# A mixture-of-experts stage behind a graph layer: its first norm moved ahead of the last edge sums, its first experts among the last dense pieces, and its later norms to the front of each VectorE step

## The reference

```python
edge_index = jnp.stack([src, dst])
xn = _layernorm(x, axis=-1)
x = x + gnn(xn, edge_index, edge_type, ...) + mix(xn[None], ...)[0]   # 2 graph layers; 4 transformer layers
x = x + ffn(_layernorm(x, axis=-1)[None], ...)[0]

def ffn(x, ...):                       # x: 3125 x 256
    all_out = experts(x)               # 4 experts: 256 -> 128 -> 64 -> 256, relu, biases eb1, eb2, eb3
    shared = shared_mlp(x)             # 256 -> 256 -> 128 -> 256, relu, biases sb1, sb2, sb3
    gates = softmax(x @ gW + gb)
    topv, topi = top_k(gates, 2)
    topw = softmax(topv)
    return shared + sum of the two chosen experts' outputs weighted by topw
```

## Time and profile before

| | before |
|---|---|
| median of 3 runs | 2031.78 us (2028.99 to 2034.85) |
| the profiled execution | 2034.2 us, span 2032.5 us |
| TensorE matmul busy | 1876.7 us (92%) |
| TensorE weight load busy | 1576.5 us (78%) |
| VectorE busy | 1260.0 us (62%) |
| ScalarE busy | 677.9 us (33%) |
| GpSimd busy | 1330.8 us (65%) |
| mean granted TensorE clock | 0.976 |

### The profile page before, as it was taken

One profiled execution on the slowest core, in us unless ns is written; L12 is line 12 of the kernel. 1 busy time (PEld: TensorE's weight loads), 2 busy tenths in 40 slices (PEclk: granted clock), 3 DMA queues, 4 the chain that ended last, 5 costly groups with the idle time before them and its releaser, 6 DMA issues.

```text
span 2032.5 us, 32105 instructions
## 1 busy us (share of the span) xinstructions
PE 1876.7 (92%) x10496; PEld 1576.5 (78%) x10496; DVE 1260.0 (62%) x3348; ACT 677.9 (33%) x1864; POOL 1330.8 (65%) x1324
## 2 busy tenths in 40 slices
PE   3989999998899999979999998798999999998878
PEld 2558888886788888759888787566888888888878
DVE  6775576566656556475567645487656566555666
ACT  5542343343234333333343333122222222223333
POOL 5777777777777777777777415776777777750000
PEclk9999999999999999999999989899999999998889
DMA  8677666667766666776666536667666666560000
GB/s 243 193 241 220 199 186 200 205 193 234 227 198 190 197 198 182 233 236 199 207 193 207 153 84 230 214 204 233 204 195 187 219 203 208 182 138 14 26 14 26
DMA packets 195288, 371.62 MB, mean 183 GB/s; under 512 B 37993, under 2 KB 126863, under 8 KB 195131
## 3 DMA queue, kind: packets, MB, share of 16 engines
q0 software_dynamic: 77376, 223.09, 38.7%
q1 hardware_dynamic: 93587, 127.50, 19.0%
q10 hardware_dynamic: 24168, 19.04, 3.2%
HBM read 305.39 MB, written 64.95 MB: 182 GB/s over the span
## 4 chain that ended last, share of the span: by engine, by line
PE 63%; POOL 13%; DVE 12%; issue 6%; DMA 3%; ACT 2%; DVEq 1%; SPq 0%; ACTq 0%
PE ps_seg L2469 12%; PE ps_down L2592 12%; PE ps_hid L2583 11%; POOL xg L906 9%; POOL rg L862 4%; PE ps_kv L2502 3%; PE ps_kv L2891 3%; PE ps_x L2547 3%; DMA xg<-h_rows,idx_tab 2%; PE ps_hid L3036 2%; PE ps_x L528 2%; DVE xg L1008 2%; PE ps_hid L2522 1%; PE ps_down L2620 1%; DVE xres L1948 1%
## 5 line engine op out<-in xcount | busy, mean ns | idle before, releaser
L906 POOL DMA_INDIRECT xg<-h_rows,idx_tab x416 | 430.9, 1036 | 140.3 <-issue 116.2
L906 POOL DMA_INDIRECT xg<-xn_rows,idx_tab x416 | 431.6, 1037 | 128.8 <-issue 122.5
L862 POOL DMA_INDIRECT rg<-relation_rows,idx_tab x416 | 430.6, 1035 | 129.4 <-issue 129.1
L2469 PE MATMUL ps_seg<-xg,hot 128*125 128x257 f32 x1664 | 428.5, 389 | 44.0 <-DVE xg L1008 43.6
L2583 PEld LDWEIGHTS ps_hid<-hT,wff 128*128 128x128 f32 x3200 | 385.1, 193 | 15.7 <-issue 7.1
L2583 PE MATMUL ps_hid<-hT,wff 128*128 128x125 f32 x3200 | 389.4, 276 | 1.6 <-ACT gT L2069 0.9
L2469 PEld LDWEIGHTS ps_seg<-xg,hot 128*125 128x125 f32 x1664 | 296.1, 190 | 102.4 <-DVE xg L1008 44.7
L2592 PE MATMUL ps_down<-wff,gT 128*125 128x256 f32 x1600 | 364.0, 381 | 0.0
L1008 DVE TENSOR_TENSOR xg<-xg,rg 128x512 f32<-128x512 f32 x416 | 285.8, 687 | 79.7 <-DMA xg<-h_rows,idx_tab 52.3
L2069 ACT ACTIVATE gT<-ps_hid,b1p 128x125 f32<-128x125 f32 x800 | 226.6, 367 | 319.9 <-PE ps_hid L2583 319.7
L2592 PEld LDWEIGHTS ps_down<-wff,gT 128*125 128x125 f32 x1600 | 295.4, 189 | 41.7
(11 more groups left out here) (367 smaller groups left out, 2424.2 us busy)
## 6 DMA issues: line engine op xcount, KB each, us to landing
second_relation_rows<-rg SPq DMA_DIRECT2D x104, 512.0 KB, 4.0
rg<-second_relation_rows SPq DMA_DIRECT2D x104, 512.0 KB, 4.2
wff<-L_mix_W ACTq DMA_DIRECT2D x8, 1024.0 KB, 7.9
rg<-relation_rows,idx_tab POOLq DMA_INDIRECT x416, 3.5
xg<-xn_rows,idx_tab POOLq DMA_INDIRECT x416, 3.2
xg<-h_rows,idx_tab POOLq DMA_INDIRECT x416, 3.7
h_rows<-rg SPq DMA_DIRECT2D x25, 112.0 KB
qrow<-h_rows ACTq DMA_DIRECT2D x25, 112.0 KB
```

The lines of the kernel that those rows point to most:

```text
L862: pool.indirect_dma_start(rg[:, k, :], None, rel_d, bass.IndirectOffsetOnAxis(ap=idx_tab[:, step, 1:2], axis=0))\
L906: pool.indirect_dma_start(xg[:, k, 0:D], None, rows, bass.IndirectOffsetOnAxis(ap=idx_tab[:, step, 0:1], axis=0))\
L2469: ins = pe.matmul(ps_seg[u // UW % 2][0:T, 0:AW], hot[:, s % HOTS, :], xg[:, s % RING, :], start=s % WIN == 0, stop=s % WIN == WIN - 1)
```

## The change

On VectorE, `last_norm(0)`, the norm of the first five tiles, is called before the flush of the last edge sums instead of behind `aside(8)`. After the loop of layers the order of what is left is `dense_beside(49)`, `(50)`, `logits(0)`, `shift_logits(0)`, `(51)`, `softmax(0)`, `(52)`, `top_two(0)`, `gates(0)`, `(54)`. The shared bias is added once to all four experts' biases (the two gate weights of a row sum to one), and `add_biases` loses its first addition; for that the expert biases are loaded to one contiguous place. In the step loop, `gates` (of the group whose tiles begin now), `last_stats`, `last_rows`, `logits` and `shift_logits` come before the step's gated rows; `gates` moves from j = 4 to the next j = 0, `logits` and `shift_logits` from j = 3 to j = 4; `softmax` and `top_two` stay at the end of j = 4.

On TensorE, `turn_last(0)` and `(1)` move before `aside(9)`; `turn_last(2)` to `(4)`, `shared_1(0)`, `experts_1(0)` and the first logits go between dense pieces 50 and 51, and pieces 52 to 54 into step s = 1. ScalarE follows the same order; it waits for the last weights before dense piece 50, and `exp_gates` stand before `columns_out` at j = 0 and before `hidden_2` at j = 4.

```diff
@@ load places
-        eb3_b = kx5p[0:T, 0:KC, 0:2 * D]
+        eb3_b = flat_k[0:T, 0:NX * D].rearrange("p (b n) -> p b n", b=KC)
+        eb3_all = flat_k[0:T, 0:NX * D].rearrange("p (e n) -> p e n", e=NX)
@@ VectorE, iteration
                 early()
                 aside(8)
-                if (lay, gi) == (L - 1, NG - 1):
-                    last_norm(0)
                 b.add_ffn(3)
@@ VectorE, early
                         if (lay, gi) == (L - 1, NG - 1):
+                            last_norm(0)
                             edges.flush()
@@ VectorE, behind the layers
             dense_beside(behind + 1)
+            softmax(0)
             dense_beside(behind + 2)
-            softmax(0)
             top_two(0)
+            gates(0)
             dense_beside(behind + 4)
-            gates(0)
@@ VectorE, step loop
-                last(dve.tensor_tensor(z, z, b2_b[:, :], ALU.add))
...
+            last(dve.tensor_tensor(eb3_all, eb3_all, b2_b[:, :].unsqueeze(1).broadcast_to([T, NX, D]), ALU.add))
             for s in range(1, NT + 2):
                 gi, j = last_part(s)
+                if j == 0 and 1 < gi <= NG:
+                    gates(gi - 1)
+                if gi < NG:
+                    if j == 0:
+                        last_stats(gi)
+                    if j == 1:
+                        last_rows(gi)
+                    if j == 4:
+                        logits(gi)
+                        shift_logits(gi)
                 if s <= NT:
                     gated_rows(s - 1)
                 if s > 1:
                     add_experts(s - 2)
                 if s <= NT:
                     add_biases(s - 1)
-                if gi < NG:
-                    if j == 0:
-                        last_stats(gi)
-                    if j == 1:
-                        last_rows(gi)
-                    if j == 3:
-                        logits(gi)
-                        shift_logits(gi)
-                    if j == 4:
-                        softmax(gi)
-                        top_two(gi)
-                        gates(gi)
+                if gi < NG and j == 4:
+                    softmax(gi)
+                    top_two(gi)
@@ ScalarE, iteration
                 aside(7)
+                if (lay, gi) == (L - 1, NG - 1):
+                    aside(8)
+                    last_turned(0)
+                    last_turned(1)
+                    aside(9)
+                    return
@@ ScalarE, behind the layers
-            last_turned(0)
-            last_turned(1)
+            last_turned(2)
+            last_turned(3)
+            act.wait_ge(s_ew, 16 * LAST_LOADS)
+            act.wait_ge(s_fo, L * NT + 1)
+            hidden_shared(0)
+            last_turned(4)
             dense_beside(behind)
-            for j in range(2, GT):
-                last_turned(j)
+            hidden_experts(0)
             dense_beside(behind + 1)
             exp_gates(0)
             dense_beside(behind + 2)
-            act.wait_ge(s_ew, 16 * LAST_LOADS)
-            act.wait_ge(s_fo, L * NT + 1)
-            hidden_shared(0)
-            hidden_experts(0)
-            dense_beside(behind + 3)
             exp_gates(1)
@@ ScalarE, step loop
                     hidden_shared(s)
+                if j == 0 and 1 < gi <= NG:
+                    exp_gates(2 * gi - 1)
                 turned(0)
...
                     hidden_experts(s)
+                if gi < NG and j == 4:
+                    exp_gates(2 * gi)
                 turned(2)
+                if s == 1:
+                    dense_beside(behind + 3)
...
-                if gi < NG and j > 2:
-                    exp_gates(2 * gi + (j - 3))
@@ TensorE, iteration
                 upto(m["ctx"])
+                if (lay, gi) == (L - 1, NG - 1):
+                    turn_last(0)
+                    turn_last(1)
                 aside(9)
@@ TensorE, behind the layers
-            turn_last(0)
-            turn_last(1)
-            dense_beside(behind, split_tile)
-            for j in range(2, GT):
-                turn_last(j)
-            dense_beside(behind + 1, split_tile)
-            last_logits(0)
+            turn_last(2)
+            turn_last(3)
             pe.wait_ge(s_ew, 16 * LAST_LOADS)
             pe.wait_ge(s_gel, L * (2 * NT) + 2)
             shared_1(0)
-            dense_beside(behind + 2, split_tile)
+            turn_last(4)
+            dense_beside(behind, split_tile)
             experts_1(0)
-            dense_beside(behind + 3, split_tile)
-            dense_beside(behind + 4, split_tile)
+            last_logits(0)
+            dense_beside(behind + 1, split_tile)
@@ TensorE, step loop
                     shared_1(s)
+                if s == 1:
+                    dense_beside(behind + 2, split_tile)
...
                 turn(2)
+                if s == 1:
+                    dense_beside(behind + 3, split_tile)
+                    dense_beside(behind + 4, split_tile)
```

## The result

The change brings 3.4 us where 15.3 were forecast: 2027.57 us (median of 20 runs, 2020.62 to 2031.85) against 2030.93 (20 runs, 2025.17 to 2036.03) for the kernel before on the same chip, ratio 0.9976 [0.9967, 0.9986]. The ratio is not the quotient of the two medians; by it the gain is 4.9 us [2.8, 6.7]. So the kernel is faster, but by less than the 0.3% that the forecast took for the least that a measurement can tell from no change, and its time lies outside the range of 2006.5 to 2022.

A forecast was written before the change was run, and what follows sets the result against it. TensorE's idle time in the last 215 us, and the half clock following it, bound the kernel. 5.0 + 30.8 - 17.2 - 8.0 + 4.2 + 0.45 = 15.25 us off 2031.8 gave 2016.5 (2012 to 2020; with rivals, 2006.5 to 2022).

The forecast's parts named there:

- The bound: TensorE sets the pace; its idle time in the last 215 us, and the half clock following it, can be won.
- Part 1, the passage: From the end of down(4) to the first layer_2: 23.90 us becomes 18.9 by interleaving, a gain of 5.0.
- rival D: Passage: x lands late, TensorE stands 13 us at turn_last(0), so nothing moves: 2029 us; chance 0.05.
- Part 2, removed: Norms of groups 1 to 4: the waits at turn_last and their half clock go, 7.7 us each, 30.8 gained.
- an undisturbed one is 6.6: Step with a group's five transposes: without the wait at turn_last it takes 6.6 us, at 0.22 per transpose.
- Part 2, added: Norm work ahead of VectorE's gated rows: new waits at turn_experts cost 17.2 us, half clock behind them 8.0.
- Rival B: Half clock in all four groups' logits steps, +3, and in the passage, +3.3: 2022.5 us; chance 0.09.
- Part 3: Gate exponentials on ScalarE: layer_3's wait at j=4 goes, at j=0 0.35 stays per group; gain 4.2 us.
- Part 4, the bias: b2 folded into the expert biases: 25 VectorE adds of 0.42 go, gaining 0.45 us at the end.
- They are hidden except at the end: VectorE's 25 bias additions cost time only at the end, where VectorE is the chain: 0.45 us.
- The signs: Trace after: four turn_experts waits of 4 to 4.6, group period 38, layer_2(0) near 1836, L528 on acc at most 0.5.
- A: Rival: new waits on turn_experts are too short to lower the clock, or come out shorter: 2006.5 to 2009 us; chance 0.22.

The follow-up runs named there:

- e8_all: Changed kernel with norm statistics spread over several steps, gate logits 64 columns wide and each group's five transposes set apart: 1989.42 us, ratio 0.9776.
- e5_bias: Kernel before with only the shared bias folded into the experts' biases: 2028.03 us against 2033.34, ratio 0.9969.
- e2_slots: Kernel before with the changed kernel's step loops (later norms' new places) and the folded bias, passage as before: 2361.57 us on another chip, ratio 0.9918.
- e10_slots_again: Same kernel as e2_slots, run again on a third chip against the kernel before: 2370.66 us, ratio 0.9957.
- e1_passage: Changed kernel with VectorE's and ScalarE's old step loops, keeping passage and folded bias: 2367.35 us against 2381.19 for the kernel before, ratio 0.9955.
- e3_root_later: Changed kernel with the norm's ten small inverse-root operations moved from step j=0 to j=1: 2358.87 us on another chip, ratio 0.9901.
- e6_wide: Changed kernel with the gate-logits matmuls 64 columns wide instead of 4: 2020.74 us, ratio 0.9938.
- e9_passage_again: Same kernel as e1_passage, run again on a third chip against the kernel before: 2368.48 us, ratio 0.9957.
- e4_spread: Changed kernel with the next group's norm sums at j=2 and root at j=3 of the group before: 2348.82 us on another chip, ratio 0.9852.

## Why the prediction was wrong, by its steps

**The bound.** TensorE's idle time in the last 215 us, and the half clock behind it, was the right thing to look at: `e8_all` takes 44.4 us out of that stretch (218.7 to 174.3), and the medians differ by 43.9 (that the two agree so well is luck: its profiled execution lies 9 us above its median).

**Part 1, the passage: right.** 5.2 measured for 5.0, with clock 1.00 in it. x was waited for 1.6 us and `turn_last(0)` 0.6, so rival D did not come; `mu_product(25)` waited 1.2 for the forecast 1.7. One pair of executions could not show this to 0.2. But the old passage took 29.5, 27.8, 30.8 and 26.6 in its four traces (before, `e5_bias`, `e2_slots`, `e10_slots_again`) and the new one 23.1 to 25.4 in five (after, `e1_passage`, `e3_root_later`, `e6_wide`, `e9_passage_again`), 4.7 less on average.

**Part 2, removed: right in kind, 4.4 us too much.** The step that failed is "an undisturbed one is 6.6". The five transposes were costed at 0.22 each as if they followed each other freely. After the change they take 7.72, because the second waits 0.70 us for ScalarE's copy of the first: all five are written to one bank. ScalarE has the two activations of `hidden_shared` ahead of that copy. In the kernel after these are still to be done when the first transpose ends; in the kernel before they were done during the large wait, and the second transpose had no wait for the copy. After, group 1, and before, group 2:

```profile
1851.34 0.62 ACT L2376 ACTIVATE gT<-ps_hid,rg 128x125 f32<-128x125 f32 x2 [2.44 <-PE ps_hid L3040]
1851.85 0.38 ACT L1986 ACTIVATE qT_all<-ps_seg 128x250 f32<-128x250 f32 x1
```

```profile
1889.17 0.62 ACT L2368 ACTIVATE gT<-ps_hid,rg 128x125 f32<-128x125 f32 x2 [2.18 <-PE ps_hid L3027]
...
1894.68 0.38 ACT L1984 ACTIVATE qT_all<-ps_seg 128x250 f32<-128x250 f32 x1 [4.89 <-PE ps_seg L528]
...
1895.21 0.65 PE L528 MATMUL ps_seg<-ident,acc 125*128 125x125 f32 x2
```

So a part of the old wait did not go with the norm, and the forecast had counted all of it. `e8_all` wins 0.85 of the 1.11 back, with the transposes in other places: 14.52 - 7.65 = 6.87 for the step and its five transposes, not the 6.6 of the forecast.

**Part 2, added: right.** Waits of 4.43, 4.37, 4.38 and 4.37 for 4.55 and 3 x 4.2. The half clock behind them was taken as 2.0 each, with 2.7 as its upper bound; in this execution it was near the bound, (50.34 - 22.44 - 17.55) / 4 = 2.6, and in `e6_wide`, with the same waits, 2.1. `e4_spread` takes out 26.5 of the 27.9. The prediction's chain of VectorE work was sound, and it could have been used one step further: the block of 4.14 us was placed where a step has 1.3 us free, plus 1.05 that the gated rows may be late. Cut into parts of some 2 us it fits, and the same trace said so.

**Rival B, more half clock in the logits steps: this came.** It was priced at +3.0 for the steps and came as 3.3, since all four take 9.28 instead of two of four. That the sum put nothing for it is the second step that failed. It stood at 0.09 because two of four in the trace before were taken as the likely state after; the forecast looked for half clock behind idle time, but in this step it goes with the twenty narrow matmuls: with 64 columns it is gone from all (`e6_wide`), and in `e4_spread`, without the large waits, two of four still have it. Its other half, half clock in the passage, did not come.

**Part 3: right in kind, but smaller than it looks.** `layer_3` is held 0.6 us instead of 5.8, and only at the end, so that the wait of j=0, which was to stay, went too. The pairs of steps j=4 and j=0 gained 1.6 each, but 0.9 of it is what `e5_bias` gives in them without Part 3; there `layer_3` is held only 2.3. That leaves 0.7 for the forecast 1.05.

**Part 4, the bias: right place, wrong size.** "They are hidden except at the end" is the third step that failed: 0.45 forecast, 5.4 or more measured when alone. It is an error on the other side, and its gain stands in the table under the steps j=4 and j=0. VectorE is idle in most steps, but an addition lies ahead of the norm, of the softmax and of the gates in the same queue, and these were waited for. The waits at `turn_last` shrank by 0.92, two additions' worth, and j=4 and j=0 by 0.46 each. The account was open to see: the prediction itself summed "time 0 at `shared_1` of step j=4" through `add_biases`.

**The parts don't add.** The fold's gain lay in waits that Parts 2 and 3 abolish anyway: in `e5_bias` the steps with the transposes are 2.9 shorter in all and the pairs j=4 and j=0 3.6, less 1.6 for the one more long logits step. Behind the first `layer_2` the stretch is 189.2 before, 183.8 with the fold alone, 183.4 and 183.2 with the fold and the new places, and 187.5 after. Against the fold alone, the new places gain nothing, and the passage ahead of them costs 4.0 at the first group. So the whole measured gain is as large as that of the fold alone, and what the passage brings, the longer first wait takes back. With the passage and the fold in place, the new places cost something: without them the last stretch is 206.8 and 204.1, with them 211.8.

**The signs.** Of those set down, these came: the four waits on VectorE's gated rows at 4.4, clock 0.58 in the window behind one, the first `layer_2` at 1836.6, and `turn_last(0)` under 1 us. These did not: the group takes 40.7 instead of 38, L528 on `acc` still waits, 0.6 once and 0.70 four times, and `layer_3` is held 0.6, not under 0.5. Some of the sums are off, none with weight: four times 0.35 is 1.4, not 1.6, and 9.9 stands 0.23 above 9.67, not 0.35; the parts of rival B add up to 2022.8, not 2022.5; those of A end at 2007.5, not 2009.

**What stays open.** The medians give 3.4, the ratio 4.9, the stretch of one pair 6.9; with executions that stray by 3 to 4 us all can hold, and no run here narrows it. Why some of the logits steps escape the half clock with 4 columns (10 of 36) isn't settled; that it is the width that lets all escape is shown by `e6_wide`. In `e8_all` the j=1 steps take 5.93 instead of 5.51, behind a wait of 0.2 for the gated rows; the rest of it was not looked into.

## What to carry to other kernels

Cost a removed wait against the step as it will run without it, and look for the next wait inside it: here 0.7 us for a copy, under a wait of 4.9. An engine that is idle on average still has a queue: whatever lies ahead of the operation that somebody waits for is paid in full, so keep for each step how long the engine is free, and cut work into parts that fit (4.1 us in one step cost 28 us in all, the same work in parts of 2 hardly any). Before reckoning a change in several parts as a sum, name the wait that each part shortens; where two name the same one, only one of them is paid.

## What the runs showed of the hardware that was not expected

**A busy TensorE can lose its clock.** In the kernel after, TensorE is busy for 9.30 of 9.30 us in the logits step, and the granted clock is 0.82: one of its two levels, 2.4 GHz, for part of the stretch and 1.2 GHz for the rest. The windows ahead of it, in group 2, from the new wait's end on:

```profile
1883.70:1889.90 6.20, 6.20 (x32) 6.17 (x33) 3.82 (x11) 1.76 (x6) 0.00 (x0) 0.58 0.36 103
...
1889.90:1898.00 8.10, 7.30 (x56) 6.74 (x56) 3.79 (x9) 3.57 (x12) 0.00 (x0) 1.00 0.01 2
```

The clock had come back, for 8.1 us with 7.3 of them busy, before it fell again in the busiest step of all. With 64 columns in place of 4 the same twenty matmuls keep 1.00. The Trainium skill, "TensorE: Matmul & The Clock Gate", Part 1, has the clock follow how busy TensorE was; in this trace it fell in a stretch without idle time, with and behind twenty matmuls of 4 columns.

**Nearly free columns.** Twenty matmuls of 128x125 weights took 2.25 us with 4 columns and 2.30 with 64.

**Chips differ.** The same kernel before took 2030.9 and 2033.3 us on two chips and 2381.2 and 2381.1 on two others. In the traces the last edge-sum matmul starts at 1811 to 1820 us on the first two and at 2141 to 2177 on the others, and the steps behind it take the same: the 350 us lie ahead of it. Why, no run shows.
